# Block rounds of a decoder's second stage on Trainium2: scatter one round later, statistics and power one block ahead, denominators on VectorE

## The reference

```
x = x + _L0_attn_ref(_layernorm(x), ...)
x = x + _L0_xattn_ref(64, 64, 256, w, u, _layernorm(x), ctx_2048)
x = x + _L0_ffn_ref(_layernorm(x), router, experts ...)
x = x + _L1_attn_ref(...); x = x + _L1_xattn_ref(...); x = x + _L1_ffn_ref(...)
```

```
y  = (A * p + E * v) / (A * q + E)
p' = A2 * p + E2 * v
q' = A2 * q + E2
```

## Time and profile before

| | |
|---|---|
| median of 3 runs | 3676.59 us |
| lowest, highest | 3674.57, 3690.04 us |
| profiled execution | 3677.66 us |
| its span | 3675.7 us, 71094 instructions |
| busy share of the span: PE, DVE, ACT, POOL | 85%, 70%, 49%, 57% |
| the stage's eight blocks, first `bn_stats` to last `sent_to` | 1548.0 to 1807.8 us |
| DMA in the span | 274.90 MB, mean 75 GB/s |

### The profile page before, as it was taken

The page is one execution under the profiler, slowest core; times in us unless marked ns, Lnnn a source line. Parts: engine busy times, 40 slices in busy tenths (PEclk is TensorE's granted clock), DMA queues, the critical chain, the costliest instruction groups (busy, mean ns, idle before and its releaser), DMA issues. The chain is left out here.

```text
span 3675.7 us, 71094 instructions
## 1 busy us (share of the span) xinstructions
PE 3132.7 (85%) x22664; PEld 2495.4 (68%) x22696; DVE 2581.5 (70%) x5658; ACT 1789.9 (49%) x3717; POOL 2096.5 (57%) x2554
## 2 busy tenths in 40 slices
PE   6789999999999999755289955788888888888888
PEld 3668888888888888644244433566766666666667
DVE  6668888888888888666433325677777777777762
ACT  5667877777877778522123322333333333333321
POOL 5666666666666666577400016666666666666660
PEclk8989999999999999977599976899999999999999
DMA  3445444444444444311111130000000000000000
GB/s 125 138 146 159 137 142 150 132 142 131 146 128 148 136 142 136 132 53 40 55 61 63 63 109 14 8 12 12 14 12 14 11 11 11 11 11 11 7 8 6
DMA packets 173790, 274.90 MB, mean 75 GB/s; under 512 B 41207, under 2 KB 107127, under 8 KB 172938
## 3 DMA queue, kind: packets, MB, share of 16 engines
q1 hardware_dynamic: 167436, 255.39, 21.6%
q0 software_dynamic: 6144, 16.79, 1.4%
HBM read 218.31 MB, written 45.39 MB: 72 GB/s over the span
## 5 line engine op out<-in xcount | busy, mean ns | idle before, releaser
L1608 POOL TENSOR_TENSOR l_prod<-l_sco,l_vE 128x256 f32<-128x256 f32 x512 | 414.8, 851 | 251.3 <-DVE l_sco L2108 251.3
L1600 POOL TENSOR_TENSOR l_prod<-l_q,l_kv 128x256 f32<-128x256 f32 x512 | 367.4, 754 | 121.2 <-DVE l_att L2116 121.2
L717 DVE SCALAR_TENSOR_TENSOR a_cq<-a_PQ,a_taps,a_cq 128x504 f32<-128x504 f32 (+2 forms) x384 | 281.8, 734 | 129.7 <-ACT a_cq L583 120.6
L717 DVE SCALAR_TENSOR_TENSOR a_ck<-a_PK,a_taps,a_ck 128x504 f32<-128x504 f32 (+2 forms) x384 | 280.8, 731 | 11.0 <-ACT a_ck L583 1.9
L341 POOL TENSOR_TENSOR a_tq<-a_cq,a_tq 128x512 f32<-128x512 f32 x128 | 165.7, 1294 | 153.6 <-ACT a_tq L589 153.6
L411 PE MATMUL a_PQ<-a_x_hi,a_wqk 128*128 (+1 forms) x512 | 202.4, 436 | 52.2 <-POOL a_wqk L292 39.1
L328 POOL TENSOR_TENSOR a_hrs<-a_hve,a_neghalf 128x8 f32<-128x8 f32 x128 | 209.4, 1636 | 22.9 <-DVE a_hve L734 22.9
L484 PE MATMUL a_Y<-a_wo,a_og_parts 128*128 128x256 f32 x1536 | 206.1, 284 | 9.4 <-POOL a_og_parts L335 9.4
L411 PEld LDWEIGHTS a_X<-a_wv,a_xb 128*128 128x128 f32 x1536 | 199.9, 188 | 12.1 <-issue 1.2
L411 PE MATMUL a_X<-a_wv,a_xb 128*128 128x256 f32 x1536 | 204.1, 282 | 0.8 <-DMA a_xb<-a_x_lo 0.8
L484 PEld LDWEIGHTS a_Y<-a_wo,a_og_parts 128*128 128x128 f32 x1536 | 194.5, 192 | 11.2 <-issue 10.2
(11 more groups left out here) (374 smaller groups left out, 8840.5 us busy)
## 6 DMA issues: line engine op xcount, KB each, us to landing
a_wqk<-qk_parts SPq DMA_DIRECT2D x112, 512.0 KB, 3.3
a_wv<-v_parts SPq DMA_DIRECT2D x56, 512.0 KB, 3.8
a_wg<-g_parts SPq DMA_DIRECT2D x112, 256.0 KB, 3.3
a_wo<-o_parts SPq DMA_DIRECT2D x112, 256.0 KB, 2.9
a_dr<-decays SPq DMA_DIRECT2D x256, 64.0 KB, 2.5
m_hs<-sorted_rows SPq DMA_DIRECT2D x72, 128.0 KB, 2.1
sorted_outs<-m_ys SPq DMA_DIRECT2D x72, 128.0 KB, 1.7
qk_parts<-a_wqk SPq DMA_DIRECT2D x16, 512.0 KB, 3.3
```

The lines of the kernel that those rows point to most:

```text
L717: nc.vector.scalar_tensor_tensor(out=acc, in0=src, scalar=taps[p][:, tap + k:tap + k + 1], in1=acc, op0=ALU.mult, op1=ALU.add).then_inc(s_ ...
L1600: nc.gpsimd.tensor_tensor(out=prod[:, h], in0=qv[:, h:h + 1, :].to_broadcast([P, H, HD]), in1=kk, op=ALU.mult).then_inc(S("E_pqk"), 1)
L1608: nc.gpsimd.tensor_tensor(out=prod[:, h], in0=sco[:, h:h + 1, :].to_broadcast([P, HD, H]), in1=vv, op=ALU.mult).then_inc(S("E_pav"), 1)
```

## The change

Three edits in the first code block of the second part, on POOL and DVE alone. PE, ACT and SP keep their orders.

1. POOL's `scatter(r)` at the end of a round becomes `scatter(r - 1)`, and the last block's scatter follows the loop.
2. `statistics(0, .)` on DVE and `power(0, .)` on POOL are done for block 0 ahead of the loop and for block f+1 at a later place in round f: on DVE between reciprocal and choice, on POOL between quotient and scatter.
3. The addition that makes `den` goes from POOL's `sums` to DVE's `scans`, between the two scans. `sums` is then called `numerator`. The first scan of a block gains a wait for the quotient of the block before, which reads `den`.

```diff
-                def sums(b):
-                    pool.wait_ge(S("fk"), b + 1)
-                    pool.wait_ge(S("qscan"), b + 1)
+                def numerator(b):
                     pool.wait_ge(S("fv"), b + 1)
-                    nc.gpsimd.tensor_tensor(out=den[:], in0=fk[:], in1=qp[:, :, 0:SEQ], op=ALU.add).then_inc(S("den"), 1)
                     pool.wait_ge(S("pscan"), b + 1)
...
+                power(0, 0)
                 for f, y, r in STEPS:
-                    if f is not None:
-                        power(0, f)
                     if r is not None:
                         power(1, r)
                     if y is not None:
-                        sums(y)
+                        numerator(y)
                     if f is not None:
                         weighted(f)
                     if y is not None:
                         quotient(y)
-                    if r is not None:
-                        scatter(r)
+                    if f is not None and f + 1 < BLOCKS:
+                        power(0, f + 1)
+                    if r:
+                        scatter(r - 1)
+                scatter(BLOCKS - 1)
...
                         dve.wait_ge(S("den"), b)
+                        dve.wait_ge(S("y"), b)
                     nc.vector.tensor_tensor_scan(out=flat(qp), data0=flat(keep), data1=flat(eh), initial=0.0, op0=ALU.mult,
                                                  op1=ALU.add).then_inc(S("qscan"), 1)
+                    dve.wait_ge(S("qscan"), b + 1)
+                    dve.wait_ge(S("fk"), b + 1)
+                    nc.vector.tensor_tensor(out=den[:], in0=fk[:], in1=qp[:, :, 0:SEQ], op=ALU.add).then_inc(S("den"), 1)
...
+                statistics(0, 0)
                 for f, y, r in STEPS:
-                    if f is not None:
-                        statistics(0, f)
                     if r is not None:
                         residual(r)
                         statistics(1, r)
                     if y is not None:
                         scans(y)
                         reciprocal(y)
+                    if f is not None and f + 1 < BLOCKS:
+                        statistics(0, f + 1)
                     if r is not None:
                         choose(r)
                         place(r)
```

## The result

The changed kernel takes 3653.78 us (median; 3637.61 to 3655.91) against 3678.25 for the kernel before in the same comparison (3673.91 to 3696.92). The ratio is 0.9911, 95% interval 0.9892 to 0.993: faster by 0.9%, more than the 0.5% that the prediction took as the least that can be told. Forecast were 3647 and a range of 3636 to 3660. The profiled execution took 3653.78 us, its span is 3652.0, and the span before was 3675.7.

The account below looks back on a forecast made before the run. A loop of waits with 12.2 us of scatter in it bounds the second stage; block gains 6.2 + 12.9 + 5.7 + 3.2 + 3.1 - 1.6 = 29.5 us give 3648.2 profiled, 3647 median, range 3636 to 3660.

Parts of the forecast that it names:

- The loop: Second stage's block round is a loop of waits, 30.7 us, with 12.2 us of unneeded scatter in its middle.
- The wait of 6.77: DVE's wait in us for POOL's denominators, forecast to go once DVE makes them itself.
- T: Moment a block's `sent_to` is ready; a round is counted from it.
- close call: Seventh scatter DMA at T+5.85 against first scan at T+5.93; any small delay was to put it into the scan.
- N: Moment POOL's `nm` is ready in a steady round, forecast T+12.9, or 11.85 if the seventh DMA slips through.
- first rival: Scans' holds on the scatter don't bite: N = T+9.8, rounds 24.4, total 3638 us; chance 0.13.
- the second: Rival: holds bite in full, N at T+15.4, rounds 28.9, total 3660 us, no change; chance 0.10.
- q: Moment POOL's quotient ends in a round, forecast N+9.85 = T+22.75.
- `ng` is held till then: DVE's `ng` was to wait for q in steady rounds, with the choice running T+22.85 to T+26.4.
- T': End of the round, when the next `sent_to` is ready, forecast q+3.6.
- The landing: Third rival: `xh` waits for queued scatter DMAs landing about T+25, total 3721 us, slower; chance 0.03.
- the rule: Skill's inference that two-input DVE instructions let scatter DMAs pass; prediction sided with the trace's holds, 2.30 and 1.91 us.

Follow-up runs that it names:

- split version: Changed kernel with numerators on DVE, scatter DMAs issued two, three and three, statistics back behind `place`, `hb` ahead of `fk`; 3643.95 us, ratio to before 0.9892.
- edits 1, 2 and 3: Three runs, each with one edit alone on the kernel before: 3657.74, 3672.30 and 3678.76 us.
- third `xh`: Changed kernel with a third `xh` buffer, so `xh` waits for a scatter one round older; 3665.63 us beside 3693.33 for the kernel before.
- denominators twice: Changed kernel with the denominators' addition done twice on DVE before the second scan; 3655.08 us.
- split version with spare transposes: The split version plus spare PE transposes ahead of `h_T` and the router's product; 3647.0 us, ratio to before 0.9893.

## Why the prediction was right, and where it was not

**By block,** gain measured (forecast): block 0 -1.13 (-1.6), block 1 +6.33 (6.2), blocks 2 to 4 +15.48 (12.9), block 5 +4.45 (5.7), block 6 +4.01 (3.2), block 7 +2.58 (3.1). The sum is 31.72 (29.5).

**The loop was read rightly.** Moving the scatter and the front power gave 3.60 a round, and POOL's queue stayed the loop. Denominators at 1.2 measured 1.23. The wait of 6.77 went. In block 1 (24.30 for 24.4) the number is partly luck: the quotient started at T+18.44 as forecast, though not because it waited for the reciprocal (T+18.18), but because POOL had waited 2.31 us for the second scan and its products ended then.

**The first round with a scatter came as written.** From block 1's `sent_to`, T = 1637.33, the seventh DMA and the power were held, by the first and the second scan, and the eighth by 0.06. The prediction's close call, a seventh DMA at T+5.85 against a scan at T+5.93, was not close here: the DMA started at T+6.49.

```profile
1643.82 2.54 POOL L942 DMA_INDIRECT sorted_rows<-m_xh,m_sent_to  x1 [0.30 <-issue]
1646.66 1.02 POOL L942 DMA_INDIRECT sorted_rows<-m_xh,m_sent_to  x1 [0.30 <-issue]
1647.69 2.22 POOL L910 TENSOR_TENSOR m_rs<-m_ve,m_neghalf 128x4 f32<-128x4 f32 x1
1649.99 0.21 POOL L912 TENSOR_TENSOR m_nm<-m_ng,m_rs 128x4 f32<-128x4 f32 x1
```

`nm` ended at 1650.20, T+12.87, where the prediction had N = T+12.9. So the first rival (no holds) fell, and the second (all of them in full, N at T+15.4) too. One sum of the prediction doesn't add up as written: 1.3, 1.37 and five times 1.27 put the seventh DMA at q+9.0 and not q+9.4. The 9.4 is right with the issue gap of about 0.5 between power and scatter that the sum leaves out: the sixth started at q+8.20 (1693.97), and one more of 1.27 gives q+9.5.

**The step that failed** is "`ng` is held till then. The choice runs T+22.85 to T+26.4", with T' = q+3.6. Of the kernel after it holds in blocks 0 and 1 alone, where `ve` comes while the quotient runs; in block 1 the quotient ran from 1631.47 to 1633.81:

```profile
1632.92 0.92 DVE L1104 TENSOR_SCALAR m_ve<-m_mv 128x4 f32<-128x4 f32 x1
1633.75 0.16 DVE L1107 TENSOR_SCALAR m_ng<-m_mv 128x4 f32<-128x4 f32 x1
```

There T' is 1637.33, q+3.52. In the steady rounds `ve` comes while `fv` still runs. By the DVE rows of the result it was held to 1709.45, `fv`'s end at 1709.43, and `ng` ran at 1709.37, at the seam before the quotient. The choice then needed only the router (1710.36) and went on under the quotient, and only its `te` ends with it: T' is 1713.87 with q at 1711.73, q+2.14, so 1.46 earlier than forecast. The kernel before had the same 2.13; the prediction used it for block 5 ("`te` is held") and not for blocks 2 to 4.

From that came the second error, of the other sign. The scatter starts where it was expected against q, but with T' earlier this is T'-0.36 and no longer about T'-1.8. From the next round on the sixth DMA too meets the first scan (1693.97, 2.95 us), the others follow it, and N comes at T+13.52 and then T+13.86, up to 1.0 later than forecast. Each round adds up from its own rows, N, then N to q, then q to T': 12.87 + 9.96 + 2.13 = 24.96, 13.52 + 9.96 + 2.13 = 25.61, 13.86 + 9.97 + 2.14 = 25.97, where the forecast had 12.9 + 9.85 + 3.6 = 26.4. In part the two errors cancel, and that is luck.

**Block 5** was forecast with 25.0, `te` held to q at T+22.75 and then 2.2 left. The mechanism came as written, the time did not: it took 26.26. N was at T+13.86, so q was at T+23.82, `te` ended with it, and 2.44 were left. DVE's missing statistics gave nothing, since the choice waited 4.26 us for the router's product, which hangs on `nm` by `xh`. In block 6 N came at T+11.31 for T+12.4, and the round was 22.64 for 23.5.

**The landing** is the rival that the profile after seemed to name, and the prediction had called it a sign of being wrong. `xh` started 0.13 us behind `nm`, not 12 us, and taking the landing away changed nothing.

**Holds against the rule.** Every DMA of the scatter that started more than 0.02 us into a scan was held, in every kernel here, and ended 0.76 us or more behind the scan: in the round of the result the sixth ended 0.76 after the first scan (1696.16) and the eighth 0.76 after the second (1699.65). The seventh, which started 0.2 before the end of the denominators, took 1.02, and so passed at the seam although the second scan followed at once. The Trainium skill (SBUF — State Buffer, Who interferes with whom) infers that a `tensor_tensor` of DVE does not hold descriptor generation, since it takes only the read side of the shared ports and descriptor generation needs the write side. The runs do not agree for these indirect DMAs: in the split version one that started beside the numerators' addition, a `tensor_tensor` with two inputs in SBUF, took 2.01 us for 0.96 and ended 0.91 behind it. Whether it is the reading of the row numbers from SBUF that is held, or something else in the DMA's issue, was not tried.

Left open is why the first stage ends up to 13 us apart in kernels that share its code. It is what keeps the total from resolving a few microseconds.

## What to carry to other kernels

An engine's idle time names a wait, not its price: the 6.77 us that DVE waited for `den`, and the landing that `xh` waited for, were each worth nothing when removed alone, and the edit that removed the first was worth 1.56 a round behind the other two. What an edit is worth in the steady rounds can also differ from its worth over a stage of eight blocks: the scatter's move gave 1.36 a round and 15.2 us in all. When an engine's own queue is the loop, count everything in it, with the holds that other engines put on it; whether a small operation gets in between two long ones decides a microsecond (2.13 or 3.5 from the quotient's end to `sent_to`), and it should be read from a row. Where totals drift by a stage that the change doesn't touch, compare the stage by its own marks.

## What the runs showed of the hardware

Whether a 4-element operation of DVE costs 0.2 us or 1.7 depends on which of POOL's back-to-back products it meets, and where in it: the waiting one (`ve`) gets in at the seam between two of them, and a second (`ng`) right behind it as well, as at 1709.4. One that comes after the seam waits out the next product, as in block 1, so a few tenths can decide a whole product. The `te` of 4 elements was held in the same way, for 1.3 us in the split version.

In block 7 of seven runs a wait stood before `rank`, with a releaser outside the core's own engines: 1.69 to 1.82 us in the repeat of the changed kernel, in the four variants of it (third `xh` to denominators twice) and, at 1.68, in the split version, and 2.61 in the split version with spare transposes. In the kernel before, the first run after and edits 1, 2 and 3 it did not. From the repeat:

```profile
1782.37 0.19 DVE L1172 TENSOR_TENSOR m_rank<-m_TY,m_base 128x32 f32<-128x32 f32 x1 [1.69 <-remote]
```

PE's matmuls for it had ended by 1780.8, so it isn't a product that is late. The cause was not found (all seven are later runs, so it need not be the kernels), and block 7 (20.15 in one run, 21.71 in the other of the same kernel) is left out of comparisons for that reason.
